# A two-layer decoder on one core: the experts' last down product in its own PSUM bank, and a reordered prologue of the state-space scan

## The reference, cut to what matters

```
# experts, second loop; z is the residual stream
h = silu(x @ w1[e]) * (x @ w3[e]);  mixed += gate[:, e] * (h @ w2[e])      # e = 0..7
z = z + mixed
# scan, on layernorm(z)
proj = x @ W_xproj;  dt, B, C = proj[:64], proj[64:80], proj[80:96]
delta = softplus(dt @ W_dt + b_dt)
dA = exp(clip(delta * A[n], -7, 20))                                       # 16 states n
S[n] = cumsum(delta * B[n] * x * exp(min(-cumsum(log dA), 20)))
y = sum_n C[n] * exp(min(cumsum(log dA), 20)) * S[n]  + x * D
```

## Time and profile before

| what | us |
|---|---|
| three runs | 563.3, 560.31, 559.34 (median 560.31) |
| the profiled execution | 559.9, of which the span of the trace is 558.2 |
| busy: TensorE, VectorE, ScalarE, GpSimd | 475.9, 448.2, 277.9, 203.8 |
| mean granted TensorE clock | 0.954 of full speed |

### The profile page before, as it was taken

One profiled execution on the slowest core, in us unless ns is written; L12 is line 12 of the kernel. 1 busy time (PEld: TensorE's weight loads), 2 busy tenths in 40 slices (PEclk: granted clock), 3 DMA queues, 4 the chain that ended last, 5 costly groups with the idle time before them and its releaser, 6 DMA issues.

```text
span 558.2 us, 9251 instructions
## 1 busy us (share of the span) xinstructions
PE 475.9 (85%) x3108; PEld 279.4 (50%) x3117; DVE 448.2 (80%) x1180; ACT 277.9 (50%) x520; POOL 203.8 (37%) x171
## 2 busy tenths in 40 slices
PE   7888999999998999899989546547579999999866
PEld 5444666666555666566655102122134656666423
DVE  7999867675587567375786999999995899998996
ACT  3840356555544244345244355555511577777655
POOL 8724000000002305332500069999990255543130
PEclk9999899999999999999999956897889999999989
DMA  5510360000010302322200000000001000000001
GB/s 148 144 42 1 95 171 2 2 1 2 1 49 9 99 11 72 115 61 59 56 1 2 1 0 0 0 0 2 0 0 47 2 2 3 1 2 2 2 0 39
DMA packets 25392, 17.34 MB, mean 31 GB/s; under 512 B 2977, under 2 KB 24162, under 8 KB 25346
## 3 DMA queue, kind: packets, MB, share of 16 engines
q1 hardware_dynamic: 24322, 14.65, 9.2%
q0 software_dynamic: 1024, 2.10, 1.3%
HBM read 10.06 MB, written 5.51 MB: 28 GB/s over the span
## 4 chain that ended last, share of the span: by engine, by line
PE 31%; DVE 21%; POOL 8%; issue 6%; ACT 3%; DMA 1%; SPq 0%; DVEq 0%; POOLq 0%; ACTq 0%
PE PS L1343 7%; PE PS L814 5%; PE PS L1385 4%; DVE PS L2249 3%; PE PS L859 3%; DVE VA L2262 3%; POOL E L2183 3%; PE PS L876 3%; POOL KSA L2175 2%; PE PS L2064 2%; DVE PS L2255 2%; POOL OT L2663 1%; POOL sorted L2653 1%; PE PS L834 1%; DMA answers<-OT 1%
## 5 line engine op out<-in xcount | busy, mean ns | idle before, releaser
L859 PE MATMUL PS<-QM,KP 32*128 32x256 f32 x512 | 91.9, 398 | 1.2 <-ACT E L1047 0.8
L814 PE MATMUL PS<-KP,QP 32*128 32x256 f32 x512 | 78.4, 404 | 0.2 <-ACT QP L1025 0.2
L1047 ACT ACTIVATE E<-PS 128x512 f32<-128x512 f32 x100 | 56.1, 595 | 34.9 <-PE PS L859 24.3
L2653 POOL DMA_INDIRECT sorted<-VA,slot_of x16 | 15.7, 979 | 145.0 <-DVE expert_at L1737 128.0
L859 PEld LDWEIGHTS PS<-QM,KP 32*128 32x128 f32 x512 | 60.6, 184 | 6.2 <-issue 4.8
L814 PEld LDWEIGHTS PS<-KP,QP 32*128 32x128 f32 x512 | 51.7, 187 | 14.6 <-issue 10.1
L1343 PE MATMUL PS<-XNT,KSA 128*128 128x512 f32 x128 | 58.6, 596 | 0.0
L1122 DVE CUSTOM_DVE_ANT_0 SCR<-PS,KSA 128x256 f32<-128x256 f32 x128 | 47.5, 420 | 9.1 <-PE PS L814 8.3
L356 PE MATMUL PS<-KSA,select 128*128 128x512 bf16 x60 | 23.6, 481 | 35.4 <-ACT KSA L2099 30.7
L1117 DVE TENSOR_REDUCE MXT<-PS 128x2 f32<-128x512 f32 x64 | 41.1, 686 | 15.5 <-PE PS L814 15.4
L2628 POOL TENSOR_TENSOR VA<-VA,KSA 128x512 f32<-128x512 f32 x28 | 35.2, 1274 | 37.7 <-ACT VA L1052 37.7
(11 more groups left out here) (340 smaller groups left out, 1013.0 us busy)
## 6 DMA issues: line engine op xcount, KB each, us to landing
KSA<-in_w SPq DMA_DIRECT2D x2, 1024.0 KB, 6.8
sorted<-zeros SPq DMA_DIRECT2D x2, 960.0 KB, 6.4
answers<-OT SPq DMA_DIRECT2D x14, 128.0 KB, 1.8
KSA<-in_w SPq DMA_DIRECT2D x2, 512.0 KB, 9.3
QP<-sorted SPq DMA_DIRECT2D x4, 256.0 KB, 3.1
QP<-sorted SPq DMA_DIRECT2D x2, 448.0 KB, 4.7
X<-in_x SPq DMA_DIRECT2D x2, 256.0 KB, 3.3
SCR<-in_ctxT SPq DMA_DIRECT2D x1, 512.0 KB, 6.1
```

Of the source, the lines that this page charges most:

```text
L814: ins = pe.matmul(score_bank(n, i)[:, q * S:(q + 1) * S], QP[rows(i), g, t:t + P], KP[rows(i), g, b * S:(b + 1) * S], start=True, stop=Tru ...
L859: ins = pe.matmul(o[:, kt * S:(kt + 1) * S], KP[rows(i), g, t:t + P], QM[rows(i), g, b * S:(b + 1) * S], start=True, stop=True, skip_group ...
L1047: act.activation(slot(m, j), drain_bank(L, m, j), ACT.Exp).then_inc(sig("exps"), 1)
```

## The change

Four things are done.

1. `down(15)` goes into bank 4 and no longer waits for `mix(14)`; `scan_delta_in` of the first half moves behind it on TensorE.
2. On VectorE the first half's row parts and `scan_positive` leave the place ahead of `mix_last`: `scan_rows_tail` now stands behind `half_residual`, `scan_positive` at the head of `scan_vector`. The filler of 20 products is split in 8 and 6 around `scan_first_row`.
3. The rounding to bf16 (to `BCM`) and the subtraction (to `BCL`) go from VectorE to GpSimd, for both halves (`scan_rows_rest`); in GpSimd's queue those of the second half stand ahead of its second `first_clamp`. The zeroing of `FLOOR` goes from VectorE to ScalarE, as a copy of zeros, ahead of the first half's softplus. The root of the second half's norm goes between the Exp and the Ln of that softplus.
4. In ScalarE's queue `scan_steps_take` of the second half goes ahead of `first_half(0)`, and `first(1)`, the first tokens of state 1, ahead of `b_copy(1)` and `c_copy(0)`.

```diff
--- before.py
+++ after.py
@@ -1357,6 +1357,12 @@
             dve.tensor_tensor(E6[:, g % 4, :], E6[:, 4 + g % 2, :], unit_bank(g, 1), ALU.mult)\
                 .then_inc(sig("gated"), 1)
 
+        LAST_DOWN = UNITS_MOE // 2 - 1
+
+        def down_bank(m):
+
+            return bank(4 if m == LAST_DOWN else 6)
+
         def pass_count(pe, k):
 
             pe.wait_ge(sig("constants"), READY["const_route"])
@@ -1376,13 +1382,13 @@
         def down(pe, m):
 
             pe.wait_ge(sig("gated"), unit_step(2 * m + 1))
-            if m:
+            if 0 < m < LAST_DOWN:
                 pe.wait_ge(sig("mixed"), mix_step(m - 1))
             if m == NE:
                 pe.wait_ge(sig("mixed"), take_step(2 * PAIRS - 1))
             for t in range(4):
                 for c in range(2):
-                    ins = pe.matmul(bank(6)[:, t * P:(t + 1) * P], E6[:, (2 * m + c) % 4, t * P:(t + 1) * P],
+                    ins = pe.matmul(down_bank(m)[:, t * P:(t + 1) * P], E6[:, (2 * m + c) % 4, t * P:(t + 1) * P],
                                     W2[:, m % NE, c, :], start=(c == 0), stop=(c == 1))
             ins.then_inc(sig("down"), 1)
 
@@ -1411,9 +1417,8 @@
                     scan_steps_in(pe, 0, SCAN_BANK[0][0])
                 if n == 14:
                     scan_rows_in(pe, 0, SCAN_BANK[0][1])
-                if n == 15:
-                    scan_delta_in(pe, 0, SCAN_BANK[0][2])
-            down(pe, UNITS_MOE // 2 - 1)
+            down(pe, LAST_DOWN)
+            scan_delta_in(pe, 0, SCAN_BANK[0][2])
 
         def tiles_tensor(pe):
 
@@ -1559,7 +1564,12 @@
                 if n == 13:
                     scan_steps_take(act, 0)
             exp_and_ln(act)
-            scan_softplus(act, ch, 0)
+            act.wait_ge(sig("gated"), unit_step(UNITS_MOE - 1))
+            ch.mark(act.activation(FLOOR.rearrange("p (k d) -> p k d", d=D),
+                                   zeros[:, :].unsqueeze(1).to_broadcast([P, T // D, D]), ACT.Copy))
+            scan_softplus_exp(act, ch, 0)
+            norm_root(act, ch, 3, tiles_of(1))
+            scan_softplus_ln(act, ch, 0)
 
         def tiles_scalar(act):
 
@@ -1812,7 +1822,7 @@
                 dve.wait_ge(sig("down"), down_step(m))
                 for t in range(4):
                     j = 4 + t
-                    ins = dve.scalar_tensor_tensor(X[:, j, :], bank(6)[:, t * P:(t + 1) * P],
+                    ins = dve.scalar_tensor_tensor(X[:, j, :], down_bank(m)[:, t * P:(t + 1) * P],
                                                    gates[:, j, m % NE:m % NE + 1], X[:, j, :], ALU.mult, ALU.add)
                 ins.then_inc(sig("x_res"), 1)
                 dve.wait_ge(sig("x_res"), 3)
@@ -1916,12 +1926,9 @@
                     scan_constants(dve, ch)
                 if n == 14:
                     scan_rows_head(dve, ch, 0)
-                if n == 15:
-                    scan_rows_middle(dve, 0)
-                    scan_rows_tail(dve, ch, 0)
-            scan_positive(dve, ch, 0)
-            mix_last(UNITS_MOE // 2 - 1)
+            mix_last(LAST_DOWN)
             half_residual(dve, ch, 1)
+            scan_rows_tail(dve, 0)
 
 
 
@@ -1978,13 +1985,18 @@
             act.wait_ge(sig("dti_psum"), half + 1)
             act.activation(DTI[:, tokens_of(half)], bank(SCAN_BANK[half][0])[0:DTR, :], ACT.Copy).then_inc(sig("dti"), 1)
 
-        def scan_softplus(act, ch, half):
+        def scan_softplus_exp(act, ch, half):
 
             x = DX[:, tokens_of(half)]
             act.wait_ge(sig("delta_psum"), half + 1)
             act.activation(x, bank(SCAN_BANK[half][2]), ACT.Abs, bias=ssmc[:, 0:1]).then_inc(sig("delta_abs"), 1)
             act.wait_ge(sig("delta_abs"), half + 1)
-            ch.link(act.activation(x, x, ACT.Exp, scale=-1.0))
+            ch.mark(act.activation(x, x, ACT.Exp, scale=-1.0))
+
+        def scan_softplus_ln(act, ch, half):
+
+            x = DX[:, tokens_of(half)]
+            ch.wait()
             act.activation(x, x, ACT.Ln, bias=1.0).then_inc(sig("delta_ln"), 1)
 
         def scan_constants(dve, ch):
@@ -2004,18 +2016,24 @@
             src = bank(SCAN_BANK[half][1])
             dve.wait_ge(sig("bc_psum"), half + 1)
             ch.link(dve.tensor_copy(BC[:, t], src))
+            if half:
+                dve.wait_ge(sig("bc_middle"), 2 * half)
             dve.tensor_tensor(BCR, src, BC[:, t], ALU.subtract).then_inc(sig("bc_read"), 1)
 
-        def scan_rows_middle(dve, half):
-            dve.wait_ge(sig("bc_read"), half + 1)
-            dve.tensor_copy(BCM, BCR).then_inc(sig("bc_middle"), 1)
-
-        def scan_rows_tail(dve, ch, half):
+        def scan_rows_rest(pool, half):
+
+            pool.wait_ge(sig("bc_read"), half + 1)
+            if half:
+                pool.wait_ge(sig("bc_rows"), half)
+            pool.tensor_scalar(BCM, BCR, 1.0, 0.0, ALU.mult, ALU.add).then_inc(sig("bc_middle"), 1)
+            pool.wait_ge(sig("bc_middle"), 2 * half + 1)
+            pool.tensor_tensor(BCL, BCR, BCM, ALU.subtract).then_inc(sig("bc_middle"), 1)
+
+        def scan_rows_tail(dve, half):
 
             t = tokens_of(half)
-            dve.wait_ge(sig("bc_middle"), half + 1)
+            dve.wait_ge(sig("bc_middle"), 2 * half + 2)
             dve.tensor_copy(BC[32:64, t], BCM[32:64, :])
-            ch.link(dve.tensor_tensor(BCL, BCR, BCM, ALU.subtract))
             dve.tensor_copy(BC[64:96, t], BCL[64:96, :]).then_inc(sig("bc_rows"), 1)
 
         def scan_positive(dve, ch, half):
@@ -2136,17 +2154,19 @@
 
             first_step(0)
             first_decay(0)
+            scan_steps_take(act, 1)
             first_half(0)
-            scan_steps_take(act, 1)
-            scan_softplus(act, ch, 1)
+            scan_softplus_exp(act, ch, 1)
+            scan_softplus_ln(act, ch, 1)
             first_step(1)
             first_decay(1)
             first_half(1)
             decay(1)
+            first(1)
             b_copy(1)
             c_copy(0)
             for n in range(NS):
-                if n + 1 < NS:
+                if 1 < n + 1 < NS:
                     first(n + 1)
                 if n + 2 < NS:
                     decay(n + 2)
@@ -2182,7 +2202,9 @@
                     pool.wait_ge(sig("summed"), n - 1)
                 pool.tensor_tensor(HC[n % 2], HH[n % 2], CCOL[n % 2], ALU.mult).then_inc(sig("outputs"), 1)
 
+            scan_rows_rest(pool, 0)
             first_clamp(0)
+            scan_rows_rest(pool, 1)
             first_clamp(1)
             pool.wait_ge(sig("dx"), 2)
             for n in range(NS):
@@ -2224,21 +2246,20 @@
                 dve.tensor_tensor_scan(CARRY[:, t], DA[0][:, t], FLOOR[:, t], 0.0, ALU.mult, ALU.add)\
                     .then_inc(sig("carried"), 1)
 
+            scan_positive(dve, ch, 0)
             scan_delta(dve, 0)
             first_log(0)
-            ch.link(dve.memset(FLOOR, 0.0))
             scan_drive(dve, 0)
             first_max(0)
             first_input(0)
             first_carry(0)
             scan_rows_head(dve, ch, 1)
             scan_positive(dve, ch, 1)
-            scan_rows_middle(dve, 1)
             scan_delta(dve, 1)
             first_log(1)
             scan_drive(dve, 1)
             first_max(1)
-            scan_rows_tail(dve, ch, 1)
+            scan_rows_tail(dve, 1)
             first_carry(1)
             first_input(1)
 
@@ -2819,8 +2840,9 @@
             self_tensor(pe)
             cross_tensor(pe, 0)
             experts_tensor(pe)
+            turn_over(pe, 1, 8)
             scan_first_row(pe, 0)
-            turn_over(pe, 1, 20)
+            turn_over(pe, 1, 6)
             half_turn(pe, 1, 5)
             turn_over(pe, 1, 2)
             scan_tensor(pe)
@@ -2839,7 +2861,6 @@
             self_scalar(act, ch)
             cross_scalar(act, ch, 0)
             experts_scalar(act, ch)
-            norm_root(act, ch, 3, tiles_of(1))
             half_take(act, 1, 5)
             scan_scalar(act, ch)
             entry_root(act, ch, 2, 0)
```

## The result

The changed kernel takes 555.96 us in the median of 6 runs (554.78 to 556.86), the kernel before 560.19 (6 runs, 558.46 to 563.3). The ratio is 0.992, with a 95% interval of 0.9896 to 0.9943. Run again on another occasion the same kernel gave 556.46 against 561.0, ratio 0.9946 (0.9916 to 0.9976). The profiled execution took 556.83 with a span of 555.1; before it was 559.9 and 558.2. So the profile has 3.07 us less, where 2.75 were forecast; both intervals stay inside 1.1%.

What follows compares the result with a forecast made beforehand. VectorE was taken to bound the stretch from the last mix to the second first_carry, VectorE and GpSimd the loop. 2.25 + 0.5 = 2.75 off 559.9 gave 557.15, said as 557.3; own range 556.4 to 558.4, wide 555.3 to 560.6.

Steps and rivals of the forecast that it cites:

- The experts' end: Last expert's four VectorE operations start at 305.07, 2.37 sooner; the scan begins at 310.17, 2.32 sooner.
- the root's gap: VectorE's 0.58 stop for the root: two row copies of 0.28 each go there, 0.05 over.
- The prologue: Start of the scan, up to the second first_carry: that carry starts at 320.85, not 323.10, 2.25 sooner; bounds 1.5 to 3.5.
- The holding: Second half of the scan's start: scan_delta(1) on VectorE is held by GpSimd's subtraction until about 318.1.
- The loop: Loop over the states: carry(1) loses its 0.83 wait; 0.5 counted in all, bounds 1.9 and below nothing.
- the other 0.4 of that sum: Loop: the unsure part of the 0.5 gain, counted beside 0.1 sure.
- The sum: Whole kernel: 2.25 before the loop plus 0.5 in it, 2.75 sooner; 557.15 from the profiled execution, said as 557.3.
- The lock: Scan's start: VectorE and GpSimd block each other on some operands; scan_delta(1), ready about 317.0, waits for the subtraction begun 316.85.
- My rival for its not being met: Scan's start: scan_delta(1) gets in first, GpSimd's subtraction waits; gain 3.5 + 0.5, about 556.0; chance 0.16.
- given back in the loop: Rival, loop: a slow gather at the end and shifted waits cost 1.5 to 2.5, about 559.3; chance 0.2.
- The last `down`: Rival, experts' end: it is late anyway behind TensorE's delta and row products, no gain, about 560; chance 0.03.
- The clock came back: Rival, loop: TensorE's granted clock stays low after the first gathers, all 15 are slow, 562.7; chance 0.06.

Runs made afterwards that it cites:

- Ln in PSUM: Changed kernel with the second half's Ln written to a PSUM bank, so scan_delta(1) reads one operand from SBUF and one from PSUM; 557.26 us, ratio 0.9946.
- the kernel before with bank 4: Kernel before with only the last down product in bank 4 and without its wait for mix(14); 560.82 us, ratio 1.0009.
- down in bank 6: Changed kernel with the last down product back in bank 6, waiting for mix(14); 559.31 us, ratio 0.9984.
- first(1) late: Changed kernel with first(1) put back behind b_copy(1) and c_copy(0); 557.36 us, ratio 0.9948.
- both fillers without the other order: Two kernels: changed kernel plus readerless TensorE products at the scan's start (557.66 us) or up to the first gather (555.93), scan_rows_head(1) not moved ahead of first_carry(0).
- FLOOR on VectorE: Changed kernel with the zeroing of FLOOR back on VectorE behind first_log(0), not on ScalarE; 559.15 us, ratio 0.9981.

## Why the prediction was right

**The experts' end.** Forecast 305.07 for the last expert's operations, measured 304.92; ScalarE had Exp done at 307.22 and waited 0.39 for the variance, so the root did not find it busy; the root's gap takes the two copies, the scan begins at 310.04 (310.17 forecast). The reason is shown: without the bank C comes 1.51 later, with the bank alone nothing moves.

**The prologue.** `first_carry(0)` at 313.51 with a wait of 0.37 (313.6 and 0.4). GpSimd's subtraction began at 316.83 (316.85) and held the addition, 1.67. The sum, 2.25, measured 2.53 on the clock of the trace and 2.47 from M to C. The holding was forecast rightly; one term was too dear, what follows the holding. The subtraction ended at 317.99, not 318.15, as it took 1.16, not 1.27. And the prediction let the whole addition start then, while a held addition needed only 0.54 more. Together 0.3: `first_max(1)` at 319.27, not 319.6, and the clamp's end at 320.53, not 320.7 to 320.95. The holding decided it: 1.67 instead of 0.69. The run with Ln in PSUM shows what it goes by for these two operations: 0.69 with one operand in SBUF and one in PSUM, and 0.47 instead of 0.19 for the next, with both in SBUF. Having only one operand in SBUF did not always keep an operation free: in the kernel before the copy at 322.49 took 0.58 instead of 0.28 beside GpSimd's clamp.

**The loop.** Here the number, 0.5, came near the measured 0.80 (0.62 in the second profile) by luck. Three statements held. "GpSimd does not start from there": its first product begins 4.18 behind C in both kernels. `clamp(2)` moved by 0.1, from 7.47 to 7.37 behind C. And VectorE's lead did next wait for GpSimd's product, 0.75. What failed is the other 0.4 of that sum: no run shows it. In its place the profiles without filler showed a first gather that did not move (17.90 behind C before, 17.88 in the changed kernel, where it took 3.62 at a granted clock of 0.50), and GpSimd's waits for gathers, 1.8 before, were 1.93, and 1.21 in the second profile, where that gather took 3.25. The loop is VectorE's own 95.86 plus its waits. The changed kernel saved the 0.83 before `carry(1)`, paid 0.75 for GpSimd's product, and had no late gather at its end, 0.71. The last is not the change's, as far as the profiles go: the kernel before with bank 4 had it too, and the changed kernel's second profile had a late gather again, 0.54. What the change itself brings in the loop is 0.83 less 0.75, 0.1; in the second profile, where that wait was 0.39, it is 0.4.

**The sum.** 2.47 of the prologue and 0.1 in the loop, 2.6, against 2.75 forecast. The two errors, 0.2 too little before the loop and 0.4 too much in it, partly cancel. The rest of the 3.1 by which the span is shorter is 0.7 of that late gather and 0.06 before M, less 0.23 behind Y. The medians are 4.2 apart in one set of runs and 4.5 in the other. Why they lie above what the profiles show is not explained; the kernel before alone has medians from 559.65 to 561.0 in its sets of runs; the interval of the second set, 0.9916 to 0.9976, takes in the 2.6, that of the first does not. As a time the median, 555.96, is 1.3 below the 557.3 forecast, below the forecast's own range of 556.4 to 558.4 and inside the wide one, 555.3 to 560.6. Of the 1.3, 0.3 is the profiled execution, 556.83 where the sum gave 557.15. The other 1.0 is where the median lies: the forecast put it 0.15 above the profiled execution, and it lay 0.87 below; in the second set it lay 0.55 above.

**The rivals.** The lock was met, by 0.03 us where 0.15 was forecast; this close, the order was not something the rows could settle, though it repeated in six profiles (the changed kernel's two, down in bank 6, first(1) late, and both fillers without the other order). My rival for its not being met, 556.0, was priced wrong: with FLOOR on VectorE the addition did get in first, and the holding went to the next operation. The gain was not given back in the loop. The last `down` was not late: it ended at 304.78, before the add of `XN` did. The clock came back after the first gather as before: 0.87 from 342 to 345 and 1.00 up to 354 (0.70 and 1.00 before).

## What to carry to other kernels

When work goes to GpSimd, look at what VectorE does at that very time: here an operation with two SBUF operands that started 0.03 after one of GpSimd's was held to its end (1.67 instead of 0.69), and for the second half the move cost more than it brought (C came 0.36 sooner without it). Move it in time, which brought 0.90 here, or put one operand in PSUM, which brought 0.73. And an edit that brings nothing alone can be worth much beside another: the bank brings 0.0 in the kernel before and 1.5 in the changed one, where the rest alone brings 0.96 and both together 2.47 (M to C). Undo each in the changed kernel and do each in the old one before judging.

## What the runs showed that I had not expected

In the runs with filler the granted clock was 1.00 as long as the filler lasted; with filler at the scan's start alone it was 0.50 from 336, 4 us after the last of it had ended (331.90), and 1.00 through 342 where it was carried on to the gather. It did not last: the third gather then took 3.13 and 3.62, at 0.60 and 0.50. This loop, in which VectorE needs 5.92 per state and GpSimd 5.85, took a gain at its head only as far as the next engine allowed: 0.83 given at `carry(1)`, 0.75 taken back at the `accumulate` of state 4, and how much went with how long the first gather took, 2.81 to 3.62 in the profiles without filler (0.75 taken back at 3.62, 0.39 at 3.25, nothing at 2.81). And thirteen profiles put M anywhere in 2.8 us, though the code up to M is the same on TensorE and VectorE, so for an edit of one microsecond the differences of marks within a trace say what medians of ten runs can't.
